# Spreading VectorE's products over three steps, and moving angle tiles to odd heads, in an attention and mixture-of-experts block

## The reference

```
mod = silu(c) @ wmod -> shift, scale and gate for both halves
h = layernorm(x) * (1 + ca) + sa
q, k, v = h @ wq, h @ wk, h @ wv          # 16 heads of 64, k and v in 4 groups
logits = h @ wr                           # 4 nodes a head; top 2 with softmax weights
pos = running count of the members of each node
for each node n:                          # rotary positions are counted inside the node
    scores = rotate(q, pos_n) @ rotate(k, pos_n).T / 8
    probs = softmax(where(causal & member_n, scores, -1e9))
    out_n = probs @ v
y = weighted sum of the two chosen nodes' out_n;  x = x + ga * (y @ wo)
h = layernorm(x) * (1 + cb) + sb
x = x + gb * (2 * p_top * expert_top1(h) + shared(h))      # gated MLPs, 7 experts
```

## Time and profile before

| | |
|---|---|
| three runs | 923.35 us median (920.02 to 923.91) |
| the profiled execution | 922.07 us, span 920.3 us |
| busy: TensorE, VectorE, ScalarE, GpSimd | 827.7, 790.6, 734.3, 607.2 us |
| mean granted TensorE clock | 0.978 of full speed |
| VectorE's reciprocals (line 1134), first and last | at 70.4 and 799.3 us |

### The profile page before, as it was taken

The page is one execution under the profiler, slowest core; times in us unless marked ns, Lnnn a source line. Parts: engine busy times, 40 slices in busy tenths (PEclk is TensorE's granted clock), DMA queues, the critical chain, the costliest instruction groups (busy, mean ns, idle before and its releaser), DMA issues. The chain is left out here.

```text
span 920.3 us, 21302 instructions
## 1 busy us (share of the span) xinstructions
PE 827.7 (90%) x6552; PEld 580.7 (63%) x6552; DVE 790.6 (86%) x1996; ACT 734.3 (80%) x2001; POOL 607.2 (66%) x951
## 2 busy tenths in 40 slices
PE   4459989999999999999999999999999999999893
PEld 4346656666666666666666666666666667575793
DVE  6869978998899889988998899889988888787895
ACT  6258898889888988898888888888888887865572
POOL 4556778776877677767776777677656666128492
PEclk9779999999999999999999999999999999999997
DMA  9101111121111121112121211121101110323553
GB/s 209 42 16 24 38 29 37 36 40 31 38 37 36 32 41 37 36 32 40 37 37 31 40 38 37 30 39 32 15 9 16 17 14 14 126 70 93 149 168 113
DMA packets 81039, 45.01 MB, mean 49 GB/s; under 512 B 35072, under 2 KB 79808, under 8 KB 80928
## 3 DMA queue, kind: packets, MB, share of 16 engines
q1 hardware_dynamic: 79712, 41.15, 20.3%
q0 software_dynamic: 1216, 2.51, 0.8%
HBM read 30.62 MB, written 12.43 MB: 47 GB/s over the span
## 5 line engine op out<-in xcount | busy, mean ns | idle before, releaser
L1543 PE MATMUL psum<-QK 128*128 128x128 f32 (+3 forms) x1024 | 369.8, 453 | 5.2 <-DMA wrow<-words 4.4
L768 ACT ACTIVATE probs<-psum,negmax 128x128 f32<-128x128 f32 (+3 forms) x512 | 266.8, 528 | 56.0 <-DVE negmax L1128 32.4
L530 POOL TENSOR_TENSOR R<-pcs 128x512 f32<-128x512 f32 x128 | 176.3, 1399 | 49.6 <-DVE pcs L1087 49.6
L1543 PEld LDWEIGHTS psum<-QK 128*128 128x128 f32 x1024 | 159.2, 192 | 51.0 <-issue 46.8
L556 POOL TENSOR_TENSOR coef<-rden,wslot 128x2 f32<-128x2 f32 x256 | 53.3, 208 | 173.4 <-DVE rden L1134 173.3
L1139 DVE SCALAR_TENSOR_TENSOR accs<-probs,coef,accs 128x128 f32<-128x128 f32 (+3 forms) x256 | 164.5, 643 | 2.5 <-ACT accs L777 2.5
L777 ACT ACTIVATE accs<-probs,coef 128x128 f32<-128x128 f32 (+3 forms) x256 | 148.0, 578 | 17.6 <-POOL coef L556 17.3
L1087 DVE TENSOR_TENSOR pcs<-psum,arena 128x512 f32<-128x512 f32 x256 | 161.7, 672 | 0.0
L1556 PE MATMUL psum<-ident,accs 128*128 128x128 f32 x640 | 115.9, 279 | 26.5 <-ACT QK L745 20.3
L1128 DVE CUSTOM_DVE_ANT_0 psum<-psum,outside 128x512 f32<-128x512 f32 x128 | 87.8, 700 | 51.9 <-PE psum L1545 51.2
L745 ACT ACTIVATE QK<-psum 128x384 f32<-128x384 f32 x235 | 116.1, 494 | 1.1 <-PE psum L1530 1.1
(11 more groups left out here) (272 smaller groups left out, 1558.2 us busy)
## 6 DMA issues: line engine op xcount, KB each, us to landing
weight_halves<-whl SPq DMA_DIRECT2D x48, 128.0 KB, 2.2
arena<-weight_halves SPq DMA_DIRECT2D x22, 256.0 KB, 3.1
wrow<-words SPq DMA_DIRECT2D x64, 86.0 KB
arena<-weight_halves SPq DMA_DIRECT2D x7, 512.0 KB, 6.7
wrow<-words SPq DMA_DIRECT2D x64, 42.0 KB
wst<-in_L_ffn_w_up_dram SPq DMA_DIRECT2D x14, 128.0 KB, 2.4
wst<-in_L_ffn_w_gate_dram SPq DMA_DIRECT2D x14, 128.0 KB, 2.4
wst<-in_L_ffn_w_down_dram SPq DMA_DIRECT2D x14, 128.0 KB, 2.5
```

Source lines behind the costliest of these rows:

```text
L530: pool.tensor_tensor(R[u][:, :, :, 0:3:2, half * HALF:(half + 1) * HALF].rearrange("p t e j f -> p (t e) j f"), halves(pc, half), halves(p ...
L768: act.activation((expB if e else expA)[:, k % (4 if e else 3), 0:w], area, ACT.Exp, scale=1.0 if k % TB < 2 else -1.0, bias=negmax[k % 4][ ...
L1543: pe.matmul(o, QK[:, u, e, rows], QK[:, u, 2, 0:w], start=True, stop=False)
```

## The change

Three things change, all inside the loop. In even heads, except those with n mod 8 = 4, the four products of head n+2 stand one in step s = 0, two in s = 1 and one in s = 2 (heads up to 58; odd heads and heads with n mod 8 = 4 keep two and two). GpSimd's part 0, which reads the products, then stands behind the coefficient of its step and no longer ahead of it. The angle tiles move from heads 0 to 3 of each eight to odd heads: 5 and 7 of one eight and 1 and 3 of the next; the first four tiles stay in heads 0 to 3, and the tile waits until the products that read the same half of the table are done. The value projection writes to a bank of the three that take turns, as a further user at s = 2, and the waits that guarded bank 7 for it go.

```diff
         def angle_tile(k):
             n, s = k // TB, k % TB
-            if s == 1 and n % SPAN < TB and n // SPAN + 1 < NH // SPAN:
-                return n // SPAN * TB + n % SPAN
-            return None
+            if s != 1 or n >= (NH // SPAN - 2) * SPAN + TB:
+                return None
+            if n < TB:
+                return n
+            return n // SPAN * TB + (n % SPAN - 1) // 2 + 2 if n % 2 and n >= SPAN - 3 else None
+
+        def spread(n):
+            return n % 2 == 0 and n % SPAN != TB
+
+        def products_at(k):
+            n, s = k // TB, k % TB
+            if n + 2 >= NH:
+                return ()
+            return (((0,), (1, 2), (3,), ()) if spread(n) else ((0, 1), (2, 3), (), ()))[s]
...
+            if k % TB == 2 and k // TB % GROUP == 2 and k // TB // GROUP + 1 < B * KV:
+                turns.append(("v", k // TB // GROUP + 1))
...
+        def value_bank(g):
+            return turn_bank(("v", g)) if g else psM
...
                 m, part = (n + 2, s - 2) if s >= 2 else (n + 1, s + 2)
-                if m < NH:
+                late = part == 0 and spread(n)
+                if m < NH and not late:
                     rotate(m, part)
                 if k >= 1:
                     coefficients(k - 1)
+                if m < NH and late:
+                    rotate(m, part)
...
+                if a >= TB:
+                    dve.wait_ge(S["prod_done"], 4 * SPAN * (a // TB))
...
-                if s < 2 and n + 2 < NH:
-                    products(n + 2, s)
+                for which in products_at(k):
+                    product(n + 2, which)
...
                 if s == 2 and n % GROUP == 2 and n // GROUP + 1 < B * KV:
-                    pe.wait_ge(S["prod_done"], 4 * (n + 3))
+                    wait_turn(pe, ("v", n // GROUP + 1))
                     project_value(n // GROUP + 1)
...
-                    pe.wait_ge(S["v_ev"], min(B * KV, (n + 2) // GROUP + 1))
```

More of the change, by code:

```diff
@@ L318, in wait_turn @@
                 kind, number = turns[i]
-                eng.wait_ge(S[{"t": "t_ev", "pt": "pt_ev", "a": "ang_abs"}[kind]], TB + 3 * number + 2 if kind == "a" else number + 1)
+                eng.wait_ge(S[{"t": "t_ev", "pt": "pt_ev", "a": "ang_abs", "v": "v_ev"}[kind]], TB + 3 * number + 2 if kind == "a" else number + 1)
         block = ctx.enter_context(nc.Block())
@@ L684, in keep_value @@
                 act.wait_ge(S["v_mm"], g + 1)
-                act.activation(v_b[:, g % 3, :, :].rearrange("p t d -> p (t d)"), psM[:, 0:TB * HD], ACT.Copy
+                act.activation(v_b[:, g % 3, :, :].rearrange("p t d -> p (t d)"), value_bank(g)[:, 0:TB * HD], ACT.Copy
                                ).then_inc(S["v_ev"], 1)
@@ L1076, in size_angles, with product @@
                                   ).then_inc(S["ang_abs"], 1)
[L1078 to L1083, removed]
-                src = psM.rearrange("p (t j f) -> p t j f", t=TB, f=HALF)
[L1085 to L1092, removed]
+            def product(n, which):
+                e, (i, dst) = which // 2, ((1, pc), (0, ps))[which % 2]
+                if which == 0:
+                    dve.wait_ge(S["qk_mm"], n + 1)
+                    dve.wait_ge(S["trig_done"], TB + 1 + 2 * (n // SPAN))
+                    if n >= 1:
+                        dve.wait_ge(S["add_done"], 2 * n)
+                src = psM.rearrange("p (t j f) -> p t j f", t=TB, f=HALF)
+                table = trig[:, n // SPAN % 2, i, n % SPAN, :, e, :]
+                dve.tensor_tensor(dst[:, :, e, :].rearrange("p t (j f) -> p t j f", f=HALF), src,
+                                  table.unsqueeze(2).to_broadcast([P, TB, 4, HALF]), ALU.mult
+                                  ).then_inc(S["prod_done"], 1)
+            for which in range(4):
+                product(0, which)
             dve.wait_ge(S["mk_t"], 3)
@@ L1098, in _ @@
             dve.tensor_reduce(lmax[:, 0, :], dif, AX_X, ALU.add).then_inc(S["w_step"], 1)
-            for e in range(2):
-                products(1, e)
+            for which in range(4):
+                product(1, which)
             dve.wait_ge(S["codes_done"], 1)
@@ L1405, in project_value @@
                 for tb in range(TB):
-                    mm_ = three(psM[:, tb * HD:(tb + 1) * HD], rows_of(b, tb),
+                    mm_ = three(value_bank(g)[:, tb * HD:(tb + 1) * HD], rows_of(b, tb),
                                 [w_v[:, l, (g % KV) * HD:(g % KV + 1) * HD] for l in range(2)], True, True)
```

## The result

The changed kernel takes 960.82 us (median of 4 runs, 958.89 to 962.08), the kernel before 922.42 (4 runs): a ratio of 1.0424, with a 95% interval of 1.0406 to 1.0442. Slower was forecast, by the right chain of waits, but 946 us; the time lies 0.8 us above the upper end of the range. The profiled span is 960.3 us, 40.0 more than before's 920.3.

What follows compares the result with a forecast made beforehand. It took ScalarE's weigh_a(4n+2), waiting for GpSimd's coefficient, to set each pair of heads; with its start at 10.6 us the terms summed to +23.4 on 922.07, 945.5, put at 946 us, range 922 to 960.

Steps and rivals of the forecast that it cites:

- The law: Pair of heads, even then odd: length is weigh_a(4n+2)'s start plus 11.97 us, or 12.32 with an odd-head angle tile.
- From the late product to weigh_a: GpSimd's parts 0 and 1 and coefficient 4.52 us, hand-over to ScalarE 0.09, disturbance by two weigh_b 0.25.
- The full locks: Rival: both weigh_b behind the late product block GpSimd fully, 0.80 us for 0.25; weigh_a at 11.14, 958 us; chance 0.12.
- The end of the late product: VectorE, step 4n+2 of spread even heads: fourth product reached 5.07 us after the pair's start, ending at 5.73.
- a lock of this kind: VectorE's wide weigh_b ahead of the late product might lose a block of 0.67 us, giving weigh_a at 9.67.
- n mod 8 = 4: Six pairs beginning with such a head: odd-head tile delays TensorE's flip, +0.4 us each, +2.4; bounds 0 and 0.5.
- Pairs without a tile: Three pairs (54, 56, 58): 22.57 us against 21.61, +0.96 each, +2.9, with weigh_a at 10.6.
- Heads 0 and 2: Their pairs keep the angle tile, now ahead of the late product: 1.32 + 0.34 us each, +3.3.
- the value's bank: Value projection in a bank of the ring: counted as nothing; 7 us at most in 15 heads if ScalarE's copy came late.
- GpSimd's wait for the reciprocal: Profile after the change: GpSimd's wait for VectorE's reciprocal would shrink; no size given.
- The rival that VectorE sets the pair: End of VectorE's even-head work decides pair length; 21.96 us with an odd-head tile, 917 to 918 us; chance 0.13.
- the absorbed case: Rival: the late product's lateness is absorbed, weigh_a(4n+2) at 9.67, sum -0.3 us, 923 us; chance 0.11.

Runs made afterwards that it cites:

- GpSimd's order alone: Changed kernel with products two and two in every head again, part 0 still behind the coefficient: 946.78 us, ratio 1.0267.
- the sooner product: Changed kernel with the late product ahead of the weigh_b and the reciprocal of its step: 973.78 us, ratio 1.0552.
- the split behind: Changed kernel with GpSimd's split of a block of weights, in spread heads, moved behind the coefficient of step 4n: 966.71 us, ratio 1.0505.
- the run without the spread: Changed kernel with products two and two and GpSimd's order as before; moved tiles and value's bank stay: 919.86 us, ratio 0.9982.

## Why the prediction was right in its mechanism and short in its size

**The law** held in every undisturbed steady pair of the three kinds: weigh_a plus 12.30 with a tile in the odd head, plus 11.96 without (forecast 12.32 and 11.97). It also held in the kernels with GpSimd's order alone, the sooner product and the split behind.

**From the late product to weigh_a** 4.86 was forecast (4.52, 0.09 and 0.25 for locks), and 371.95 - 367.01 = 4.94 came. The locks cost about what was taken: line 553 took 1.27 in place of 1.04. The full locks behind the product, 0.80, did not come. As a mechanism that rival fell; its 958 came near the time by other sums.

**The end of the late product was mis-sized**, 5.73 against 6.09: this is the step that failed inside the pair. I took the first part of VectorE's order to be what it was before, less one product. But that product had covered the row maximum's wait for the scores (0.16 now), and without it weigh_b came 1.52 after the start of the pair and not 1.86, right as GpSimd's multiplication began. GpSimd and VectorE, timelines in the pair of head 30 before the change, which starts at 414.80:

```profile
416.28 0.63 POOL L546 TENSOR_TENSOR kwork<-ktoks,code 128x256 f32<-128x256 f32 x1
...
416.66 0.66 DVE L1139 SCALAR_TENSOR_TENSOR accs<-probs,coef,accs 128x384 f32<-128x384 f32 x1
```

So of the 0.60 taken out, 0.26 was lost ahead of weigh_b (0.16 of it is that wait) and 0.34 in the longer weigh_b itself (1.00 for 0.66); the one of 512 columns gave 0.24 back (0.74 for 0.98), which leaves the 0.36. I had put a lock of this kind on the weigh_b of 512 columns and as a gain only; it fell on the one of 384 as a loss. Moving the split gave back 0.28 of the 0.36 on that term. In the 17 pairs where a block of weights is split, at some 0.3 each, it is about 5 of the 6.6 us by which the terms were short. The Trainium skill (page "SBUF — State Buffer", section "Who interferes with whom") has the instruction that comes second wait for the whole of the first. The trace agrees but for the last 0.2: line 564 had 0.59 left to run when weigh_b started, and weigh_b took 0.39 more than the 0.61 that it takes while GpSimd does nothing (at 703.23).

**The clock had no term** in my sum, and this is the larger omission, 9.9 of 18 us, or 11.7 with the pair of head 4. I forecast the later start of TensorE's transposes without asking what TensorE does meanwhile: it is idle some 2 us, and the matmuls behind that ran at about half the rate in six pairs more than before.

**The smaller terms.** n mod 8 = 4: 0.33 a pair, forecast 0.4. Pairs without a tile: 3.4 without the clock, forecast 2.9, since weigh_a starts there at 10.7 and not at 10.6. Heads 0 and 2 4.5, forecast 3.3: I had left out the value's bank, which with the tile in an even head costs 1.0. That it costs nothing was wrong as a statement and right for 14 of its 15 places.

**GpSimd's wait for the reciprocal** grew, and I had said it would shrink. Moved ahead of part 0, the coefficient of step 4n+1 meets its reciprocal 2.3 us too early; what had filled that time, part 0, now stands behind it. The run with GpSimd's order alone shows that this suffices for 0.85 of the 1.35 a pair. My chain had only the product's place as a cause; that its sum came near all the same is luck, since the late product ends later still and hides what the order costs.

**The rival that VectorE sets the pair** has its number in the run without the spread: 21.95 in all three kinds, for 21.96. The law gives the same there (9.63 + 12.32), so that run does not tell the two apart. In the changed kernel weigh_a starts at 11.0, and the rival fell.

**A slip in a rival's sum.** In the absorbed case the three pairs without a tile would be 0.03 longer (9.67 + 11.97 against 21.61) and not 0.06; its -0.3 becomes -0.4, and no chance hangs on it.

## What to carry to other kernels

Ask of an in-order engine what it does while its next instruction waits: a small instruction with a late input, put ahead of a long one whose inputs are ready, moves the long one to that input's time. When an instruction is taken out from ahead of others, price what it had covered (the wait of the next, and whom that one now meets), and do so with each condition that the moved work waits for, not only the one that was moved. And when a step makes TensorE wait longer at one place, look at the granted clock behind the wait as well.

## What the runs showed of the hardware

TensorE's granted clock fell from 2.4 to 1.2 GHz behind idle times of 1.94 to 2.63 us, in a loop in which the engine was otherwise busy nearly all the time (21.21 of 23.30 us in the pair of head 42), and stayed there for a stretch of 3.4 us, at a cost of 1.6 to 1.7 us in each of six pairs. The same idle time in other pairs (2.13 in that of head 24, 1.95 in that of head 42, 2.63 in that of head 10) was followed by no fall. Matmuls that nobody reads, in the place of the idle time, kept the clock at 2.4 GHz behind the pair of head 4.

What a VectorE instruction with two SBUF inputs loses to GpSimd depends on where in GpSimd's instruction it begins. The weigh_b of 128x384 takes 0.61 us while GpSimd does nothing. It took 1.00 when it began 0.03 us into the multiplication of part 3 (362.44 behind 362.41); in the kernel before it took 0.86 when it began 0.17 into the same one (148.56 behind 148.39), and 0.66 when it began 0.38 into it (416.66 behind 416.28). Offset and loss add up to 0.42, 0.42 and 0.43, so an estimate from these rows is that it is held until 0.42 us into an instruction of 0.62. GpSimd loses too: its next instruction, the second of part 3, took 0.92 behind the multiplication at 416.28, and 0.73 in the run with the split behind (361.97).
